# Two GNN layers with LayerNorm on one core: another order of the casts in pass 0, the normalisation of x1 on VectorE, the maximum of the scores by way of TensorE, and the second unit's M3 and M4 around M7

## The chip, the cores and the metric

One core of one Trainium2 chip. The metric is the device time of one execution in microseconds (us); less is better.

## The reference, cut to what matters

Inputs: x (4096 x 256, f32) and adj (4096 x 4096, f32, zeros and ones, symmetric), and small weights. `ln` is a LayerNorm over the 256 columns without affine part.

```python
deg = max(sum(adj != 0, axis=1), 1);  dinv = rsqrt(deg)
x1  = ln(x + relu((dinv * (adj + I) * dinv @ x + x) @ W0 + b0))
h   = x1 @ W_sa;   s_left = h @ a[:256];  s_right = h @ a[256:]
e   = where(adj != 0, exp(-leaky_relu(s_left[:, None] + s_right[None, :], 0.01)), 0)
x_a = (e / (e.sum(1) + 1e-5)) @ h
x_b = adj @ (x1 @ W_gcnb) + b_gcnb
g_a = sigmoid([adj @ x1, x1] @ Wa.T + ba);  g_b = the same with Wb and bb
out = ln(x1 + sigmoid(g_a * x_a + g_b * x_b))
```

`node_degree` of the first layer is `deg`, so the node factors reduce to a division by `deg`.

## The kernel before, in words

A program with one instruction stream for each engine, written out by hand; semaphores (`S[...]`) order the streams, and each stream does its instructions strictly in the order written. The 4096 rows are 32 tiles of 128 (t or n).

**Pass 0 (to 61.9 us).** For each tile t TensorE transposes x (`xt_step`) and multiplies by W0 (`z_step`); ScalarE copies the transpose out of PSUM (`xt_copy`, L523), ScalarE (tiles below `ZACT`) or VectorE copies the product z (`z_copy`, L528, L824). Both split z into two f16 halves `y` (`y_hi` on ScalarE, L535; `y_lo` on VectorE, L851), which waits for a scale (`sx_ready`) that needs all of x. `z_step(t)` waits for `xt_copy(t)`, and z lies in two alternating banks. From the 14th turn on TensorE adds, in each of 16 turns, one row block of adj times y for the first four output tiles (`pass0_rows`, L1324); the other row blocks follow at the end.

**Strips and casts.** adj arrives on SP's queue as 128 strips of 512 KB (L336; 16 strips are a quarter, that is the columns of four output tiles). A strip is cast to one byte an element (`cast`: even strips by ScalarE, L515, odd ones by VectorE, L811). Six strips fit (`RING`): strip s is requested when strip s - 6 is cast. Behind strip `WTS_AT` SP requests all weights of the second layer (`load_weights`, 12 DMAs, four of them of single elements and five broadcasts to all partitions, L307 to L317). Behind strip 21, SP writes the first quarter's codes to DRAM (2 x 1 MB, L324) once strips 0 to 15 are cast; the strips from 22 on are requested behind that.

**Pass 1 (to 328 us).** For each output tile n TensorE sums 64 products (`sum_tile`, L1324; the first four tiles take theirs in pass 0), and between quarters of a tile it transposes an older tile of x1 (`t_step`, L1344) and projects it (`p_step`, L1359). VectorE makes x1 (`degree`, `residual`, `stats`); GpSimd takes the power for the standard deviation (L438) and the shift (L441), ScalarE normalises (`normalize`, L551). ScalarE's `x1t_copy` and `proj_copies` and VectorE's `x1t_lo`, `h_lo` and `forms_lo` split the results into halves.

**Attention.** 16 units of 256 rows. A unit u has seven products after Strassen (M1 to M7, `product`, L1417) for x_b, in banks 0 to 3 (M3 and M5 in 0, M4 and M2 in 1, M1 and M7 in 2, M6 in 3; of unit 0, M5 and M2 in banks 4 and 7), and four chunks of weights times h (`e_chunk`, L1468) for x_a. A chunk c goes: ScalarE's 8 exponentials (`exp_chunk`, L637), VectorE's `mask_chunk` (L1083), ScalarE's `high_chunk` (L646), VectorE's `low_chunk` (L1090), TensorE's `e_chunk`. Products are read by ScalarE (`low_m34`, `low_m1`, `low_m52`, `low_m67`) and VectorE (`middle`: M3 and M4; `middle_m1`; `sums_52`; `sums_67`). TensorE's order of unit 0 to 1 is: M7 of unit 0, then `free_products` (M3, M4 of unit 1, waiting for `sums_52`), `outer_products` (M1, M6), e chunk 0, `onto_products` (M2, M5), e chunk 1, `last_product` (M7 of unit 1, waiting for `middle_m1(1)`), e chunks 2 and 3. The exponentials need `slb`, which needs the maximum of the scores over all rows (`nmax`): GpSimd's `partition_all_reduce`, L450. `row_factors` (L1060 to L1072) gives `slrow` and `arg_ready`, for which ScalarE waits (`rr`, L751).

Of the kernel before, what the change touches and what calls it, by code (L numbers as in the profile page):

```python
# [88 lines left out]
def build(nc, x, adj, W0, b0, Wsa, asa, Wg, bg, Wa, ba, Wb, bb, out):  # L89
# [121 lines left out]
    with ExitStack() as ctx:  # L211
# [196 lines left out]
        def _(pool):  # L408
# [99 lines left out]
        def _(act):  # L508
# [39 lines left out]
            def normalize(n):  # L548

                act.wait_ge(S["shift_ready"], n + 1)  # L550
                act.activation(x1[:, n % X1RING, :], x1[:, n % X1RING, :], ACT.Identity, scale=lnst[:, n % 2, RS],  # L551
                               bias=lnst[:, n % 2, SHIFT]).then_inc(S["x1_ready"], 1)
# [1017 lines left out]
```

## Time and profile before

| | |
|---|---|
| median of 3 runs | 886.35 us (885.96 to 887.74) |
| the profiled execution: its time, its span | 885.95 us, 884.1 us |
| TensorE (PE) busy | 857.5 us, 97% |
| VectorE (DVE) busy | 660.2 us, 75% |
| ScalarE (ACT) busy | 588.4 us, 67% |
| GpSimd (POOL) busy | 208.0 us, 24% |
| mean granted clock of TensorE | 0.991 |

Times are us from the start of the span. A row of a timeline has start, duration, engine, line and operation, output <- inputs, and the idle time of the engine before it with what ended it; consecutive like instructions are merged. TensorE works without a break from 112 to 341 us and from 351 us to 877 us.

### The profile page before, as it was taken

The numbers are of one execution on the slowest core, as the hardware profiler recorded it, in microseconds if no ns is written. First come the engines' busy times: TensorE is split into PE (matmuls) and PEld (weight loads), VectorE is DVE, ScalarE is ACT, GpSimd is POOL, SyncE is SP. The second block draws the span as 40 slices with busy tenths as digits, with TensorE's granted clock in tenths as the row PEclk, the third lists the DMA queues.
The fourth block names the chain that finished last, engine by engine and source line by source line (L and its number), as shares of the span: only waits on it lengthen the run. The fifth ranks groups of instructions, "written<-read, shape, count | busy, mean of one in ns | idle before, by whom it ended". The sixth has DMA issues, their size and how long they took to land.

```text
span 884.1 us, 20483 instructions
## 1 busy us (share of the span) xinstructions
PE 857.5 (97%) x7573; PEld 756.1 (86%) x7573; DVE 660.2 (75%) x1146; ACT 588.4 (67%) x1246; POOL 208.0 (24%) x217
## 2 busy tenths in 40 slices
PE   7998899999999997999999999999999999999996
PEld 6887788888888885888888888888888888888886
DVE  5697465556465457898889988978978978978863
ACT  4664555655555436889877966967967867867832
POOL 1023244343433330110122022032032032032031
PEclk9999999999999999999999999999999999999999
DMA  9789999999989615101220220220220220220001
GB/s 323 226 318 328 340 352 349 382 299 347 364 299 362 217 55 193 54 8 49 79 79 1 77 77 9 68 77 0 77 77 0 77 77 0 77 77 0 25 24 37
DMA packets 67690, 130.02 MB, mean 147 GB/s; under 512 B 6544, under 2 KB 30128, under 8 KB 63152
## 3 DMA queue, kind: packets, MB, share of 16 engines
q1 hardware_dynamic: 58704, 120.87, 39.0%
q10 hardware_dynamic: 8928, 8.38, 2.9%
q8 instruction: 36, 0.59, 0.3%
q14 instruction: 22, 0.18, 0.1%
HBM read 99.87 MB, written 29.36 MB: 146 GB/s over the span
## 4 chain that ended last, share of the span: by engine, by line
PE 90%; DMA 3%; DVE 3%; ACT 1%; SPq 1%; issue 1%; POOL 1%; ACTq 0%; POOLq 0%; DVEq 0%
PE ps L1468 38%; PE ps L1324 22%; PE ps L1417 22%; PE ps L1359 5%; DMA strip<-in_adj_dram 2%; PE ps L1307 1%; DMA xs<-in_x_dram 1%; PE ps L1344 1%; SPq L330 0%; DVE sc L818 0%; PE ps L1296 0%; ACT codes L515 0%; SPq L312 0%; DVE ec L1083 0%; POOL fs L274 0%
## 5 line engine op out<-in xcount | busy, mean ns | idle before, releaser
L1468 PE MATMUL ps<-fb,em 128*128 128x257 f16 x3072 | 347.5, 273 | 0.0
L1468 PEld LDWEIGHTS ps<-fb,em 128*128 128x128 f16 x3072 | 300.5, 98 | 37.4
L1324 PE MATMUL ps<-y,codes 128*128 128x257 f16 x2048 | 238.7, 274 | 0.0
L1324 PEld LDWEIGHTS ps<-y,codes 128*128 128x128 fp8e4 x2048 | 200.9, 98 | 27.2 <-issue 0.3
L637 ACT ACTIVATE ec<-slb,nsb 128x256 f32<-128x256 f32 x512 | 210.8, 496 | 0.1
L1090 DVE SCALAR_TENSOR_TENSOR em<-ec,em 128x2048 f16<-128x2048 f32 x64 | 147.4, 2303 | 24.6 <-ACT em L646 24.6
L646 ACT ACTIVATE em<-ec 128x2048 f16<-128x2048 f32 x64 | 122.0, 1908 | 62.5 <-PE ps L1468 57.1
L1083 DVE SCALAR_TENSOR_TENSOR ec<-ec,pan 128x2048 f32<-128x2048 f32 x64 | 146.7, 2292 | 3.2 <-issue 1.8
L461 POOL TENSOR_TENSOR sc<-sc,sc 128x2 f32<-128x2 f32 x15 | 38.6, 2572 | 245.2 <-DVE sc L1178 245.2
L1417 PE MATMUL ps<-zz,dd 128*128 128x256 f16 x768 | 89.4, 273 | 1.4 <-DVE t L1112 1.4
L1417 PEld LDWEIGHTS ps<-zz,dd 128*128 128x128 fp8e4 x768 | 75.1, 98 | 10.4 <-DVE t L1112 1.7
L515 ACT ACTIVATE codes<-strip 128x1024 uint8<-128x1024 f32 x64 | 66.8, 1048 | 8.6 <-DMA strip<-in_adj_dram 7.0
L455 POOL TENSOR_TENSOR w<-w,bgb 128x512 f32<-128x512 f32 x16 | 27.9, 1744 | 175.8 <-DVE w L1140 156.9
L1417 PE MATMUL ps<-fa,pan 128*128 128x260 f16 x512 | 62.6, 282 | 5.2 <-DVE s L1120 3.9
L944 DVE SCALAR_TENSOR_TENSOR dd<-pan 128x512 uint32<-128x512 uint32 (+2 forms) x85 | 64.2, 815 | 0.0
L551 ACT ACTIVATE x<-x,lnst 128x256 f32<-128x256 f32 x32 | 19.2, 600 | 67.4 <-POOL lnst L441 67.4
L1417 PEld LDWEIGHTS ps<-fa,pan 128*128 128x128 fp8e4 x512 | 51.3, 100 | 13.7 <-issue 4.2
L1417 PE MATMUL ps<-fa,dd 128*128 128x260 f16 x512 | 59.5, 274 | 0.4 <-DVE m L1102 0.4
L438 POOL TENSOR_TENSOR lnst<-lnst,sc 128x1 f32<-128x1 f32 x32 | 27.2, 850 | 137.5 <-DVE lnst L988 134.7
L960 DVE TENSOR_SCALAR lnst<-ps 128x1 f32<-128x1 f32 x32 | 5.0, 157 | 72.2 <-PE ps L1324 72.2
L1417 PEld LDWEIGHTS ps<-fa,dd 128*128 128x128 fp8e4 x512 | 49.9, 98 | 7.3 <-issue 0.6
L1359 PE MATMUL ps<-wps,x1t 128*128 128x256 f16 (+1 forms) x384 | 48.6, 277 | 6.8 <-DVE x1t L950 6.8
(149 smaller groups left out, 808.8 us busy)
## 6 DMA issues: line engine op xcount, KB each, us to landing
strip<-in_adj_dram SPq DMA_DIRECT2D x128, 512.0 KB, 7.1
a_scratch<-codes SPq DMA_DIRECT2D x16, 1024.0 KB, 9.7
pan<-a_scratch SPq DMA_DIRECT2D x16, 1024.0 KB, 5.1
x_scratch<-x ACTq DMA_DIRECT2D x32, 128.0 KB, 5.2
x1r<-x_scratch SPq DMA_DIRECT2D x16, 256.0 KB, 2.8
h_scratch<-hst ACTq DMA_DIRECT2D x30, 136.0 KB, 5.5
out_dram<-ot SPq DMA_DIRECT2D x15, 256.0 KB, 2.2
fb<-h_scratch SPq DMA_DIRECT2D x3, 1088.0 KB, 8.7
```

Of the source, the lines that this page charges most:

```text
L455: pool.tensor_tensor(w[:], w[:], bgb[:].unsqueeze(1).broadcast_to([P, 2, D]), ALU.add).then_inc(S["bias_ready"], 1)
L461: pool.tensor_tensor(sc1[:, RS2], sc1[:, VE2], sc[:, MH2], ALU.pow).then_inc(S["yrstd_ready"], 1)
L515: act.activation(codes_of(s), strip_of(s), ACT.Copy, scale=float(EDGE - NONE), bias=float(NONE)).then_inc(S["cast_act"], 1)
L637: e_ = act.activation(ec[:, c % ER, jj, :], slb[:, slot, :], ACT.Exp, scale=-(1 - SLOPE), bias=nsb[:, jb:jb + 1])
L646: act.activation(em[:, c, 0], ec[:, c % ER], ACT.Copy, scale=MU / EDGE_VAL).then_inc(S["ehigh_ready"], 1)
L944: return dve.scalar_tensor_tensor(out=o, in0=b, scalar=0x7f7f7f7f, in1=a, op0=ALU.bitwise_and, op1=ALU.bitwise_xor)
L1083: dve.scalar_tensor_tensor(out=ec[:, c % ER], in0=ec[:, c % ER], scalar=1.0, in1=pan[:, slot, c * CH:(c + 1) * CH, :].bitcast(F8), op0=ALU ...
L1090: dve.scalar_tensor_tensor(out=em[:, c, 1], in0=ec[:, c % ER], scalar=MU / EDGE_VAL, in1=em[:, c, 0], op0=ALU.mult, op1=ALU.subtract).then ...
L1324: mm = pe.matmul(ACC(n), codes[:, qq % SLOTS, h, jb, e * P:(e + 1) * P].bitcast(F8), y[:, jb, part, 0:YC], start=(jb == 0 and part == 0), ...
L1359: mm = pe.matmul(b, x1t[:, n % 2, x_part, k * P:(k + 1) * P], wps[:, k, w_part, c0:c1], start=(k == 0 and x_part + w_part == 0), stop=(k = ...
L1417: mm = pe.matmul(ps[:, bank, 0:2 * c], a.bitcast(F8), g, start=(p == 0), stop=(p == NP - 1))
L1468: mm = pe.matmul(PH(2 * m + e)[:, 0:HC], em[:, c, e_part, i, e * P:(e + 1) * P], fb[:, jb, h_part, 0:HC], start=(jb == 0 and e_part + h_pa ...
```

## The change

- Pass 0: `ZACT` is 12 (z_copy of tiles 10 and 11 by ScalarE; y starts at turn 12, with 1.5 tiles a turn in place of 2). Casts at ScalarE's turns 11, 13, 14, 16, 17, 19, ... and VectorE's 12, 14, 15, 17, 18, ...: 14 and 13 in pass 0 in place of 11 and 10. The weights are requested behind strip 6 (8 before); VectorE's work on them begins at turn 22 (18 before).
- x1 is normalised by one VectorE instruction, subtract and multiply, that waits for GpSimd's power; GpSimd's shift and ScalarE's instruction go. The same for the last two output tiles.
- ScalarE's part of the forms (`forms_hi`) goes from the end of `proj_copies` behind the next `x1t_copy`. The orders of both engines in tiles 4 and 5 change with the casts.
- `nmax`: TensorE transposes the column of maxima, broadcast, into bank 5 behind M2 of unit 0, and VectorE reduces it; then `slb` ahead of `forms_lo(15)`.
- Unit 0: TensorE does M3 of unit 1, M7 of unit 0, M4 of unit 1. ScalarE's reads of products go between the first exponentials. VectorE's order changes; `row_factors` is split, and `arg_ready` comes behind `mask_chunk(0, 0, 1)`.

```diff
-ZACT = 10
+ZACT = 12
-WTS_AT = 8
+WTS_AT = 6
@@ gpsimd
                 pool.tensor_tensor(ln[:, RS], ln[:, VE], sc[:, MH], ALU.pow).then_inc(S["rstd_ready"], 1)
-                pool.wait_ge(S["rstd_ready"], n + 1)
-                pool.tensor_scalar(ln[:, SHIFT], ln[:, RS], ln[:, 6:7], -1.0, ALU.mult, ALU.mult ...
-            pool.wait_ge(S["nsr_max"], 1)
-            pool.partition_all_reduce(sc[:, NMAX], sc[:, NM], P, RMAX).then_inc(S["nmax_ready"], 1)
@@ split_at
-            upto = lambda i: 0 if i < ZACT else min(i - 1, 2 * (i - ZACT) + 2)
+            upto = lambda i: 0 if i < ZACT else min(i - 1, 3 * (i - ZACT) // 2 + 2)
@@ scalar, pass 0
-                if t >= 11 and t % 2 == 1:
+                if t == ZACT - 1 or t > ZACT and t % 3 != 0:
                     cast(1)
@@ scalar, tiles 0 to 5 (the new order)
+            cast(1); x1t_copy(0); cast(1); proj_copies(0); x1t_copy(1); cast(1)
+            proj_copies(1); x1t_copy(2); forms_hi(0); cast(1); proj_copies(2); x1t_copy(3)
+            cast(1); proj_copies(3); cast(1)
@@ scalar, unit 0
-            low_m34(0)
-            low_m1(0)
             act.wait_ge(S["slb_ready"], 2)
-            exp_chunk(0, 0, 0, first=True)
-            exp_chunk(0, 0, 1, first=True, behind={6: lambda u: low_m52(u, first=True)})
+            exp_chunk(0, 0, 0, first=True, behind={4: low_m34, 5: low_m1, 7: lambda u: low_m52(u, first=True)})
+            exp_chunk(0, 0, 1, first=True, behind={6: lambda u: low_m67(u, first=True)})
             high_chunk(0, 0, True)
-            low_m67(0)
+            act.wait_ge(S["m52_read"], 1)
+            low_m34(1)
             act.wait_ge(S["arg_ready"], 1)
             act.activation(rr[:], tb[:], ACT.Exp).then_inc(S["rr_ready"], 1)
             high_chunk(0, 1, True)
-            low_m34(1)
             exp_chunk(0, 0, 2, first=True)
@@ vector, pass 0
-                if t >= 12 and t % 2 == 0:
+                if t % 3 != 1:
                     cast(1)
@@ vector, tiles
+            def normalize(n):
+                ln = lnst[:, n % 2, :]
+                dve.wait_ge(S["rstd_ready"], n + 1)
+                dve.tensor_scalar(x1[:, n % X1RING, :], x1[:, n % X1RING, :], ln[:, 6:7], ln[:, RS], ALU.subtract,
+                                  ALU.mult).then_inc(S["x1_ready"], 1)
@@ vector, behind the last tile
+            dve.wait_ge(S["nmt_done"], 1)
+            dve.tensor_reduce(sc[:, NMAX], ps[:, 5, P:2 * P], AX, ALU.max).then_inc(S["nmax_ready"], 1)
             ... slb, then forms_lo(NP - 1) and the last differences (these two stood ahead of slb)
@@ vector, unit 0
             middle(0)
             middle_m1(0)
-            row_factors()
-            dve.wait_ge(panel_in[1], 16)
             some_differences(1, 1, DIFF_ORDER[0:2], done=4)
             mask_chunk(0, 0, 0)
+            read_67(0)
+            row_ends()
+            read_52(0, first=True)
-            sums_52(0, first=True)
+            low_chunk(0, 0)
+            add_52(0, first=True)
+            add_67(0)
+            some_differences(1, 1, DIFF_ORDER[2:], done=NPROD + 1)
             mask_chunk(0, 0, 1)
-            sums_67(0)
-            low_chunk(0, 0)
-            some_differences(1, 1, DIFF_ORDER[2:])
+            row_factors()
             middle(1)
             low_chunk(0, 1)
@@ tensor
+            pe.wait_ge(S["nsr_max"], 1)
+            pe.transpose(ps[:, 5, P:2 * P], sc[:, NM].broadcast_to([P, P]), ident[:]).then_inc(S["nmt_done"], 1)
             product(0, "M5", 0, early, bank=FIRST_52[0])
+            pe.wait_ge(S["mid_read"], 1)
+            pe.wait_ge(panel_in[1], 16)
+            product(1, "M3")
             pe.wait_ge(S["mid_read"], 2)
             product(0, "M7")
+            product(1, "M4")
-            free_products(0, 0, 1)
             pe.wait_ge(S["hlo_ready"], T)
             outer_products(0, 0)
+            pe.wait_ge(S["m52_read"], 1)
+            pe.wait_ge(S["slrow_ready"], 1)
```

`row_ends` is h_lo of the last tile and `slrow`; `read_52` and `read_67` are the PSUM reads of `sums_52` and `sums_67`, and `add_52` and `add_67` the rest of them.

## Rows read from the trace of the kernel before

**Rows 1.** TensorE's waits, whole span: us in total, times, longest.
```profile
PE ps L1359 <- DVE x1t L950: 6.8, 3, 3.5
```
**Rows 2.** Timeline of TensorE, pass 0 and tile 4.
```profile
21.57 1.62 PE L1307 MATMUL ps<-w,xt 128*128 128x256 f32 x4 [2.96 <-ACT xt L523]
...
25.45 1.07 PE L1324 MATMUL ps<-y,codes 128*128 128x257 f16 x8
...
56.53 1.04 PE L1324 MATMUL ps<-y,codes 128*128 128x257 f16 x8
...
61.70 14.24 PE L1324 MATMUL ps<-y,codes 128*128 128x257 f16 x128
...
86.52 2.41 PE L1359 MATMUL ps<-wps,x1t 128*128 128x262 f16 x12 [3.53 <-DVE x1t L950]
```
**Rows 3.** Timeline of ScalarE, pass 0 and tile 4.
```profile
20.36 0.91 ACT L535 ACTIVATE y<-zf,sc 128x256 f16<-128x256 f32 x2 [2.64 <-DVE sc L845]
...
44.37 1.06 ACT L515 ACTIVATE codes<-strip 128x1024 uint8<-128x1024 f32 x1 [1.17 <-DMA strip<-in_adj_dram]
...
82.83 1.06 ACT L515 ACTIVATE codes<-strip 128x1024 uint8<-128x1024 f32 x1 [3.54 <-DMA strip<-in_adj_dram]
```
**Rows 4.** Timeline of SP's queue: the first of the weights.
```profile
28.45 0.99 SPq L307 DMA_DIRECT2D wp<-in_L_gnn_W_gcnb_dram  x2
```
**Rows 5.** Chain of waits in order of time, strips 10 and 30: start, duration.
```profile
34.93 9.42 DMA strip<-in_adj_dram
...
78.08 4.72 DMA strip<-in_adj_dram
```
**Rows 6.** L336 from 57.7 to 57.8, strip 22: issue (ns, start), then landing.
```profile
L336 SPq DMA_DIRECT2D strip<-in_adj_dram x1: 1539/1539/1539, 57.8 to 57.8; - x1
...
DMA to landing us min/median/max: 11.2/11.2/11.2
```
**Rows 7.** Timeline of TensorE, first units.
```profile
350.97 6.43 PE L1417 MATMUL ps<-fa,pan 128*128 128x260 f16 x32 [3.94 <-DVE s L1120]
...
360.74 5.44 PE L1468 MATMUL ps<-fb,em 128*128 128x257 f16 x48
...
374.84 1.91 PE L1417 MATMUL ps<-zz,dd 128*128 128x256 f16 x16
```
**Rows 8.** Busy by engine in one stretch; the number behind POOL is the granted clock.
```profile
353.00:354.00 1.00, 1.00 (x7) 0.67 (x6) 0.92 (x2) 0.29 (x1) 0.00 (x0) 0.50 0.00 0
```
**Rows 9.** Timeline of GpSimd, behind the last tile.
```profile
342.59 0.42 POOL L450 PARTITION_ALL_REDUCE sc<-sc  x1 [9.09 <-issue]
```
**Rows 10.** Timeline of ScalarE, first units.
```profile
340.59 0.51 ACT L594 ACTIVATE zz<-fs 128x384 f16<-128x384 f32 x1
...
343.67 5.69 ACT L637 ACTIVATE ec<-slb,nsb 128x256 f32<-128x256 f32 x14
...
357.81 3.30 ACT L637 ACTIVATE ec<-slb,nsb 128x256 f32<-128x256 f32 x8
...
366.94 3.69 ACT L646 ACTIVATE em<-ec 128x2048 f16<-128x2048 f32 x2
```
**Rows 11.** Timeline of VectorE, first units.
```profile
345.43 0.40 DVE L1060 TENSOR_SCALAR rab<-ex,sc 128x32 f32<-128x32 f32 x2
...
347.99 2.28 DVE L1083 SCALAR_TENSOR_TENSOR ec<-ec,pan 128x2048 f32<-128x2048 f32 x1
...
354.06 0.42 DVE L1138 TENSOR_TENSOR s<-s,t 128x256 f32<-128x256 f32 x1
...
357.07 1.89 DVE L944 SCALAR_TENSOR_TENSOR dd<-pan 128x512 uint32<-128x512 uint32 x3
...
371.50 0.29 DVE L1112 TENSOR_TENSOR t<-ps,t 128x128 f32<-128x128 f32 x1
```
**Rows 12.** Timeline of GpSimd, last tile.
```profile
881.07 0.26 POOL L481 TENSOR_SCALAR sc<-sc 128x1 f32<-128x1 f32 x1
```
**Rows 13.** Timeline of ScalarE, last tile.
```profile
881.37 0.60 ACT L794 ACTIVATE ot<-sg,sc 128x256 f32<-128x256 f32 x1 [2.35 <-POOL sc L481]
```

More of the change, by code:

```diff
@@ L546, in _ @@
                 y_hi(t)
[L548 to L552, printed above, removed]
             def x1t_copy(n):
@@ L705, in low_m52, with low_m67 @@
                 a_.then_inc(S["low_m52"], 1)
-            def low_m67(u):
-                gate(act, S["prod_done"], u * NPROD + NPROD, "passed_act")
+            def low_m67(u, first=False):
+                gate(act, S["prod_done"], u * NPROD + NPROD + first, "passed_act")
                 gate(act, S["mid_read"], u * 2 + 2, "passed_act")
@@ L789, in _ @@
                 act.activation(sg[:, e, :], sg[:, e, :], ACT.Tanh, scale=sc[:, HINVA]).then_inc(S["sigmoid_ready"], 1)
-                act.wait_ge(S["yshift_ready"], NPAN + e)
-                if e == 0:
-                    act.wait_ge(out_sent, 16 * (NPAN - 1))
-                c, b = RS2.start + e, SH2.start + e
-                act.activation(ot[:, e, :], sg[:, e, :], ACT.Identity, scale=sc1[:, c:c + 1], bias=sc1[:, b:b + 1]
-                               ).then_inc(S["out_ready"], 1)
         @block.vector
@@ L999, in _ @@
             cast(1)
+            normalize(0)
             head(1)
             x1t_lo(0)
-            cast(2)
+            normalize(1)
+            cast(1)
             head(2)
-            cast(2)
+            h_lo(0)
+            normalize(2)
+            x1t_lo(1)
+            cast(1)
             head(3)
-            h_lo(0)
-            x1t_lo(1)
-            cast(3)
             h_lo(1)
+            x1t_lo(2)
+            normalize(3)
             forms_lo(0)
-            x1t_lo(2)
+            cast(1)
             h_lo(2)
             x1t_lo(3)
+            cast(2)
             head(4)
-            cast(2)
+            h_lo(3)
+            normalize(4)
+            cast(1)
             for n in range(PT + 2, T + 3):
@@ L1036, in _ @@
                 if more:
-                    cast(2)
+                    cast(1)
+                if n - 1 < T:
+                    normalize(n - 1)
+                if more:
+                    cast(1)
                 if T - 2 <= n <= T:
@@ L1054, in _, with row_ends @@
             dve.tensor_scalar(slb[:], slb[:], sc[:, NMAX], None, ALU.min).then_inc(S["slb_ready"], 1)
+            forms_lo(NP - 1)
+            for op in DIFF_ORDER:
+                difference(0, op, NP - 2, NP).then_inc(S["diff_ready"], 1)
+            def row_ends():
+                h_lo(T - 1)
+                dve.wait_ge(S["slt_done"], 1)
+                dve.tensor_scalar(slrow[:], ps[0:T, 5, 0:P], sc[0:T, NMAX], None, ALU.min
+                                  ).then_inc(S["slrow_ready"], 1)
             def row_factors():
-                h_lo(T - 1)
                 for c in range(2):
@@ L1123, in sums_52, with add_52 @@
                 s_.then_inc(S["m52_read"], 1)
+            def add_52(u, first=False):
+                wq = w[:].rearrange("p e (h c) -> p (e h) c", c=P)
                 if not first:
@@ L1207, in attend_tile @@
                 dve.tensor_scalar(one(VE2), two(MV2, 2)[:, e, 1:2], EPS, None, ALU.add).then_inc(S["ystat_ready"], 1)
+                dve.wait_ge(S["yrstd_ready"], NPAN + e)
+                if e == 0:
+                    dve.wait_ge(out_sent, 16 * (NPAN - 1))
+                dve.tensor_scalar(ot[:, e, :], sg[:, e, :], two(MV2, 2)[:, e, 0:1], one(RS2), ALU.subtract, ALU.mult
+                                  ).then_inc(S["out_ready"], 1)
             def dve_step(s, m, nth, ramp=False):
```

90 lines of the change are left out of this document (41 added, 49 removed).

## The prediction, on record before the changed kernel ran

> **What bounds the kernel now.** I read the busy shares first, then TensorE's waits, then the timelines around them. TensorE is busy for 97% of the span and from 112 us on nearly without a break, so a change pays only where TensorE stands still or is slow. The waits show three such places: in pass 0 before 62 us; in tiles 4 to 6, three waits for `x1t_lo` of 6.8 us together [rows 1]; and between pass 1 and the attention, one of 3.94 us with a clock at 0.50 behind it, so that 32 matmuls take 6.3 us (350.97 to 357.24) where the chunk of 48 in 5.44 says 3.6 [rows 7, 8]. The longest of the three in tile 4 (3.53 us, [rows 2]) ends when ScalarE has a strip: its cast at 82.83 waited 3.54 us for DMA with `x1t_copy` behind it [rows 3]. The last tile's chain behind TensorE is the fourth place [rows 12, 13]. Steady state elsewhere gives nothing.
>
> **Pass 0, start.** ScalarE stands before its first y_hi until the scale comes, at 20.36 [rows 3], with `xt_copy(11)` behind it; TensorE waits 2.96 us for that and then runs slowly [rows 2]. With `ZACT` 12 two more tiles pass before y_hi, and TensorE meets the wait only at the first `pass0_rows`, which start at 21.7 (y_hi and y_lo, 0.45 each, after 20.36, and their hand-overs) in place of 25.45 [rows 2]. From there a turn takes 1.97: the 15 turns from 25.45 to 56.53 are 31.1 with 1.1 of waiting and some slack in them [rows 2].
>
> **Pass 0, weights.** The first cast no longer stands behind y_hi and is done near 20, so the weights are requested at 20.2 in place of 28.45 [rows 4]. Strips behind them are late: strip 10, the second behind the weights, was requested at 34.93 and landed 9.42 later, while one on an empty queue needs 4.7 [rows 5]. ScalarE's cast of it shows what follows: 1.17 of idleness and the next `xt_copy` behind it [rows 3]. Now strips 7 and 8 stand there. Moved with the weights, strip 8 lands at 44.35 - 8.25 = 36.1. Ends: 31.4 (requested 26.7, plus 4.7) and 38 (four strips of 1.3 are still in the queue at 20.2). I take 36.1. ScalarE wants it in turn 17, at 29.6; `xt_copy(18)` is then done at 37.4, and TensorE, there at 32.7, does `z_step(18)` at 37.5: a wait of 4.8, where before the weights cost 1.1. The slow stretch behind it costs 1.9 (as 21.57 to 25.45, 3.88 for a turn of 1.97, [rows 2]). `pass0_rows` end at 37.5 + 1.75 + 1.9 + 9 x 1.97 = 58.9; before 57.4.
>
> **Pass 0, end.** Before, ScalarE cast 11 strips here, now 14, up to strip 26. Strips from 22 on are requested behind the two writes of codes. Strip 22 landed at 57.76 + 11.2 = 69.0 [rows 6], 12.6 after strip 21 was requested (56.4); no one wanted it in pass 0. Now strip 21 is requested when VectorE has cast strip 15 (turn 23), about 51.5; strip 22 lands at 64.1, or 1 earlier as fewer strips are ahead: 63. ScalarE wants it in turn 28, near 58. `z_step(29)` starts at 64.4, `z_step(30)` behind strip 24 (65.7, a cast of 1.0 and a copy) at 67.0, and the long sum at 69.0 in place of 61.8 [rows 2]: +7.2. Idle stretches between 60 and 67 slow its start: +1.5 (nothing to 1.9). Together +8.7; if strip 8 comes at 31.4 and DMA never pauses, the strips still let the sum begin no earlier than 61.5, so the lower end is 0; the upper is 10.5.
>
> **Tiles 4 to 6.** In exchange 27 strips are cast before, the rest have landed long before they are wanted, and ScalarE's and VectorE's order puts one cast, not two or three, before each copy TensorE waits for: -6.8 [rows 1], and -1.6 for the slow clock behind the 3.53 (the 12 matmuls at 86.52 take 2.41, at 0.11 each they would take 1.3, and the next lose 0.5, [rows 2]). VectorE now waits in line for GpSimd's power (0.3 to 0.9 a tile) and `forms_hi(0)` for GpSimd's sums ahead of `proj_copies(2)`; I count 1.0 for small waits in tiles 5 and 6 (0 to 2.5). Normalising costs VectorE 0.4 a tile beside 8.6 us of TensorE: nothing in steady state; if VectorE were full it would be 27 x 0.4 = 11. Sum of pass 0 and 1: 8.7 - 8.4 + 1.0 = **+1.3**.
>
> **The maximum.** GpSimd's answer came at 343.01 [rows 9]; a transpose (0.3) and a reduction (0.3) at 339.4 let `slb` be ready at 340.9, and the first exponential starts when `forms_hi(15)` ends, 341.1 [rows 10], in place of 343.67.
>
> The Trainium skill (VectorE: DVE Perf Modes, "Why tensor_reduce can't reduce along partition axis") sends a reduction over partitions to GpSimd, since VectorE's lanes don't talk to each other. Going by that rule alone the exponentials would stay at 343.67 and the forecast would move 2.5 later at most; the row, 4 us from VectorE's maximum to GpSimd's end, speaks for the transpose.
>
> **First units.** An exponential is 0.406 (5.69 for 14, [rows 10]). Chunk 0 with three reads in it is done at 345.5, chunk 1 at 349.1, high part (3.69 for two) at 351.0, low part (2.2, like the mask at 347.99, [rows 11]) at 353.2. TensorE has M3 of unit 1 at 343.9, M7 of unit 0, M4, M1, M6 to 352.9, without a slow clock: its e chunk 0 starts at 353.3 in place of 360.74 [rows 7], 7.4 ahead. That lead is then lost. Behind the low part VectorE has now the sums (1.4: four of 0.42 and a small one, as 354.06), three differences (1.9), the mask of chunk 1 (2.2) and `row_factors` (1.1: 345.43 to 346.8 without `slrow`) [rows 11]: `arg_ready` at 359.8. ScalarE waits for exactly that from 351.3, in front of high part 1 and exponentials 2, for which nothing is missing. Before, that mask and the factors were done by 353.6. Exponentials of chunk 2 start at 359.8 + 0.2 + 1.85 = 361.9 in place of 357.81 [rows 10]. From there to the end of `middle_m1(1)` took 371.79 - 357.81 = 14.0 [rows 10, 11], one chain without slack: exponentials 2 and 3, gates, high part 2 (366.94), low part 2, the two additions. Now it ends at 375.9. TensorE is through e chunk 1 at 369.5 (begun at 364.2), stands 6.4 us at M7 of unit 1, and starts it at 375.9, before at 375.0 [rows 7]: +0.9. The clock falls as after 3.94 us; there it cost 6.3 - 3.6 = 2.7; I take 2.4 (1.6 to 2.8). **+3.3**, ends 0 and +5. Later chunks were ready 5.5 us or more before TensorE came, and VectorE is now 4.1 later, so no further wait.
>
> **Last tile.** GpSimd's 0.26 and its hand-over go, and ScalarE's 0.60 becomes about 0.43 on VectorE [rows 12, 13]: **-0.5**.
>
> **Sum.** 1.3 + 3.3 - 0.5 = +4.1 on the profiled 885.95 (span 884.1 and 1.85 around it): 890.05. That execution lies 0.4 below the median of 886.35, so the median comes to 890.5.
>
> **Rivals.** (1) *Pass 0 isn't held up.* If the weights pass in the shadow of the queue and the writes of codes don't delay strip 22 (strips land near 31.4 and 56), pass 0 ends where it did, and 8.4 of waits in tiles 4 to 6 go: 885.95 - 7.4 + 3.3 - 0.5 = 881.4, or 881.8. For it: the queue ran empty before the weights. Against: 9.42 behind them [rows 5]. It decides when strip 22 lands before 59. (2) *The lead at the first units is kept*, because VectorE reaches `arg_ready` before ScalarE needs it: 890.5 - 3.3 - 7.4 = 879.8. For it: chunk 0 starts early. Against: 8.6 us of VectorE's work stands ahead of it in the new order. (3) *Both losses are half the size* (strip 22 at 60.5, M7 no later and 1 us of slow clock): 886 to 887. (4) *More waits*: VectorE, 4 us late in the units, misses the 5.5 us, and casts wait again for codes in tile 5: +9 to +11, 896.
>
> **How the numbers follow.** No change is within 0.2% (1.8 us). Chances: the forecast 0.50, (1) 0.16, (2) 0.08, (3) 0.15, (4) 0.11. Faster is (1) and (2), 0.24; the same (3), 0.15; slower 0.61. The forecast's own range is 888.3 to 893.5. The range from 882.5 to 895.5 takes in (3) and the near parts of (1) and (4).
>
> **What would show it.** Right: a wait of TensorE near 33 and one near 61 us ended by ScalarE's `xt_copy`, behind casts ended by DMA; the long sum at 69; no wait longer than 1 us from tile 4 to 6; ScalarE idle for 8 us from 351 (all behind pass 0 shifted by 1.3), ended by VectorE; TensorE idle for 6 us before M7 of unit 1, clock 0.50 behind it. Wrong: pass 0 ending by 63, or e chunk 2 of unit 0 starting earlier than 376.

## The result

The changed kernel takes **892.56 us** (median of 5 runs, 892.13 to 894.18); the kernel before took 885.96 us beside it (5 runs, 884.71 to 887.74). The ratio is **1.0078**, with a 95% interval of 1.0061 to 1.0095: slower by about 6.6 us. The forecast was 890.5, that is 4.1 slower. The profiled execution took 892.56 us with a span of 890.3 (before 885.95 and 884.1), so the spans differ by 6.2 us.

Three points of TensorE divide that difference: the start of the long sum that ends pass 0, the start of the late part of unit 0's M3 (the first product behind pass 1), and the end of the span.

| us | before | after | difference | forecast |
|---|---|---|---|---|
| long sum starts | 61.70 | 71.49 | +9.8 | +8.7 (7.2, and 1.5 for a slow start of the sum) |
| late M3 of unit 0 | 342.42 | 344.23 | +1.8 | +1.3 |
| from there to the end | 541.7 | 546.1 | +4.4 | +2.8 |
| of it behind the last group of 192 matmuls of TensorE | | | -0.55 | -0.5 |
| of it the first units | | | +4.9 | +3.3 |

### The profile page after: what moved, and what is told of

It is laid out like the page before. It is cut to its first block, busy times and chain, and to the rows that moved or that the text cites. A ratio compares the mean times of both kernels' runs of the same rounds, so it can differ in the third digit from the quotient of the medians.

```text
span 890.3 us, 20447 instructions
## 1 busy us (share of the span) xinstructions
PE 861.1 (97%) x7574; PEld 758.1 (85%) x7574; DVE 686.0 (77%) x1179; ACT 570.4 (64%) x1214; POOL 183.1 (21%) x182
## 4 chain that ended last, share of the span: by engine, by line
PE 77%; issue 8%; DVE 6%; ACT 5%; POOL 2%; DMA 1%; POOLq 0%; SPq 0%; ACTq 0%; DVEq 0%
PE ps L1498 29%; PE ps L1346 21%; PE ps L1439 18%; PE ps L1381 4%; ACT ec L622 3%; PE ps L1329 3%; ACT em L631 1%; DVE ec L1084 1%; DVE dd L921 1%; DVE em L1091 1%; DMA strip<-in_adj_dram 1%; PE ps L1366 1%; PE ps L1318 1%; POOL zb L431 0%; PE ps L1309 0%
## 5 line engine op out<-in xcount | busy, mean ns | idle before, releaser
L1346 PEld LDWEIGHTS ps<-y,codes 128*128 128x128 fp8e4 x2048 | 200.7, 98 | 28.6 <-DVE y L828 1.8
L449 POOL TENSOR_TENSOR w<-w,bgb 128x512 f32<-128x512 f32 x16 | 26.1, 1634 | 192.4 <-DVE w L1151 192.4
L1439 PE MATMUL ps<-fa,dd 128*128 128x260 f16 x512 | 61.3, 279 | 3.0 <-DVE m L1103 3.0
L1439 PE MATMUL ps<-fa,pan 128*128 128x260 f16 x512 | 60.0, 274 | 1.4 <-DVE zz L907 1.1
L545 ACT ACTIVATE x1t<-ps 128x256 f16<-128x256 f32 x32 | 12.3, 384 | 73.0 <-PE ps L1366 73.0
L438 POOL TENSOR_TENSOR lnst<-lnst,sc 128x1 f32<-128x1 f32 x32 | 25.2, 789 | 149.5 <-DVE lnst L965 149.5
L788 DVE TENSOR_SCALAR codes<-strip 128x1024 uint8<-128x1024 f32 x64 | 50.1, 785 | 1.9 <-DMA strip<-in_adj_dram 1.9
L560 ACT ACTIVATE q<-ps,sc 128x1 f32<-128x1 f32 x32 | 11.2, 351 | 62.9 <-PE ps L1381 62.9
## 6 DMA issues: line engine op xcount, KB each, us to landing
a_scratch<-codes SPq DMA_DIRECT2D x16, 1024.0 KB, 10.2
```

Of the source, the lines that this page charges most:

```text
L788: dve.tensor_scalar(codes_of(s), strip_of(s), float(EDGE - NONE), float(NONE), ALU.mult, ALU.add).then_inc(S["cast_dve"], 1)
L1346: mm = pe.matmul(ACC(n), codes[:, qq % SLOTS, h, jb, e * P:(e + 1) * P].bitcast(F8), y[:, jb, part, 0:YC], start=(jb == 0 and part == 0), ...
L1439: mm = pe.matmul(ps[:, bank, 0:2 * c], a.bitcast(F8), g, start=(p == 0), stop=(p == NP - 1))
```

## The profile after

TensorE's waits over the whole span (us in total, times, longest). They answer to [rows 1]: the three waits for `x1t_lo` are down to 0.3, and others stand in their place.

```profile
PE ps L1329 <- ACT xt L514: 9.9, 5, 4.9
PE ps L1439 <- DVE t L1113: 4.8, 1, 4.8
PE ps L1439 <- DVE m L1103: 3.2, 3, 2.4
```

TensorE's timeline in pass 0 and tiles 4 to 6, the rows that answer to [rows 2]:

```profile
22.34 1.05 PE L1346 MATMUL ps<-y,codes 128*128 128x257 f16 x8 [0.98 <-DVE y L828]
...
37.59 2.08 PE L1329 MATMUL ps<-w,xt 128*128 128x256 f32 x4 [4.16 <-ACT xt L514]
...
66.07 2.08 PE L1329 MATMUL ps<-w,xt 128*128 128x256 f32 x4 [4.92 <-ACT xt L514]
...
68.78 2.66 PE L1329 MATMUL ps<-w,xt 128*128 128x256 f32 x8 [0.21 <-ACT xt L514]
...
103.34 1.50 PE L1381 MATMUL ps<-wps,x1t 128*128 128x262 f16 x12 [0.33 <-DVE x1t L927]
...
108.63 0.44 PE L1366 MATMUL ps<-ident,x 128*128 128x128 f32 x2 [0.28 <-DVE x L971]
```

ScalarE's timeline has the cause of both waits, as [rows 3] had for tile 4. Each stands behind a cast that waited for its strip, strip 8 and strip 22, with the next `xt_copy` queued behind it:

```profile
36.22 1.06 ACT L506 ACTIVATE codes<-strip 128x1024 uint8<-128x1024 f32 x1 [5.86 <-DMA strip<-in_adj_dram]
...
64.70 1.06 ACT L506 ACTIVATE codes<-strip 128x1024 uint8<-128x1024 f32 x1 [5.38 <-DMA strip<-in_adj_dram]
65.67 0.35 ACT L514 COPY xt<-ps 128x256 f32<-128x256 f32 x1
```

SP's queue shows what stood before these two strips. The weights [rows 4] are issued from 20.34 on, and for 7.8 us no strip is requested; the codes are written at 53.15.

```profile
20.34 0.98 SPq L307 DMA_DIRECT2D wp<-in_L_gnn_W_gcnb_dram  x2
...
28.17 24.87 SPq L336 DMA_DIRECT2D strip<-in_adj_dram  x15
53.15 0.88 SPq L324 DMA_DIRECT2D a_scratch<-codes  x2
54.07 6.08 SPq L336 DMA_DIRECT2D strip<-in_adj_dram  x5
```

Busy time by stage of the same kernel (window; PE, PEld, DVE, ACT, POOL busy and count; granted clock, DMA share, GB/s). Two columns matter. TensorE is busy for 3.15 of the 8 us from 58 to 66, while DMA is full (1.02). Then, from 72 to 90, TensorE is full and DMA is at 0.52, since a strip is requested when one is cast, and only four are cast in that time. Before, DMA stood at 0.69 from 50 to 58 and at 0.91 from 72 to 90.

```profile
50.00:58.00 8.00, 8.00 (x60) 6.88 (x59) 6.71 (x22) 5.90 (x13) 0.00 (x0) 1.00 1.00 355
58.00:66.00 8.00, 3.15 (x21) 2.48 (x20) 7.15 (x10) 2.47 (x6) 3.85 (x1) 0.83 1.02 400
...
72.00:90.00 18.00, 18.00 (x166) 16.01 (x165) 15.32 (x44) 3.77 (x9) 4.90 (x7) 1.00 0.52 180
```

TensorE's timeline of the first units, which answers to [rows 7]. The products come at once, e chunk 0 starts at 355.44 in place of 360.74 though pass 1 ended 1.8 later, and then the lead goes: 2.37 us for `middle(1)`, slow matmuls (32 in 5.37, elsewhere 3.71), 4.77 us for `middle_m1(1)`, slow matmuls again. The first slow stretch costs nothing: in e3, below, the same wait of 2.37 is followed by 3.71 us for the 32, the next wait is 6.05, and M7 of unit 1 starts as far behind M3 of unit 0 (34.5 us, here 34.4).

```profile
355.44 5.44 PE L1498 MATMUL ps<-fb,em 128*128 128x257 f16 x48 [0.42 <-DVE em L1091]
...
363.25 5.37 PE L1439 MATMUL ps<-fa,dd 128*128 128x260 f16 x32 [2.37 <-DVE m L1103]
...
378.67 3.57 PE L1439 MATMUL ps<-zz,dd 128*128 128x256 f16 x16 [4.77 <-DVE t L1113]
```

The granted clock behind the longer wait, same columns as above, as in [rows 8]:

```profile
380.00:384.00 4.00, 4.00 (x21) 2.75 (x20) 3.69 (x6) 4.00 (x12) 0.00 (x0) 0.50 0.00 0
```

ScalarE starts the exponentials early (the counterpart of [rows 10]) and is then idle for 9.72 us, until VectorE's last row factor, `tb`:

```profile
342.81 1.69 ACT L622 ACTIVATE ec<-slb,nsb 128x256 f32<-128x256 f32 x4
...
362.62 0.23 ACT L735 ACTIVATE rr<-tb 128x32 f32<-128x32 f32 x1 [9.72 <-DVE tb L1073]
362.75 1.89 ACT L631 ACTIVATE em<-ec 128x2048 f16<-128x2048 f32 x1
```

VectorE, which ScalarE waits for (the counterpart of [rows 11]): low part, sums, three differences, mask of chunk 1, row factors, from 352.89 to 362.58 without a break.

```profile
352.89 2.29 DVE L1091 SCALAR_TENSOR_TENSOR em<-ec,em 128x2048 f16<-128x2048 f32 x1 [1.18 <-ACT em L631]
...
356.37 2.96 DVE L921 SCALAR_TENSOR_TENSOR dd<-pan 128x512 uint32<-128x512 uint32 x3
359.26 2.28 DVE L1084 SCALAR_TENSOR_TENSOR ec<-ec,pan 128x2048 f32<-128x2048 f32 x1
361.46 0.39 DVE L1064 TENSOR_SCALAR rab<-ex,sc 128x32 f32<-128x32 f32 x2
...
362.39 0.19 DVE L1073 TENSOR_TENSOR tb<-tb,ta 128x32 f32<-128x32 f32 x1
```

And the last tile on VectorE, in place of [rows 12, 13]:

```profile
887.77 0.41 DVE L1226 TENSOR_SCALAR ot<-sg,sc 128x256 f32<-128x256 f32 x1 [0.68 <-POOL sc L473]
```

## The experiments

Nine kernels, all edits of the changed one. The times are medians; the three right columns are read from one profiled execution of each kernel. "M3" is the start of the late M3 of unit 0, "rest" the time from there to the end of the span. All results together:

| kernel | median us | ratio to before (95%) | long sum | M3 | rest |
|---|---|---|---|---|---|
| before | 885.96 | | 61.70 | 342.42 | 541.7 |
| changed | 892.56 | 1.0078 (1.0061 to 1.0095) | 71.49 | 344.23 | 546.1 |
| e1: row factors early | 887.51 | 1.0018 (1.0005 to 1.0032) | 70.36 | 342.73 | 540.7 |
| e2: and ScalarE's wait for them later | 885.98 | 1.0004 (0.9992 to 1.0015) | 72.35 | 344.68 | 539.4 |
| e3: casts and weights as before | 882.22 | 0.9956 (0.9943 to 0.9970) | 58.75 | 334.08 | 546.1 |
| e4: codes behind strip 27 | 890.21 | 1.0054 (1.0033 to 1.0075) | 66.22 | 340.98 | 546.0 |
| e5: weights behind strip 16 | 902.97 | 1.0195 (1.0174 to 1.0215) | 72.92 | 354.85 | 546.0 |
| e6: e2 and e3 together | 876.53 | 0.9899 (0.9875 to 0.9923) | 58.42 | 334.79 | 539.5 |
| e7: e3, weights behind strip 6 | 882.15 | 0.9958 (0.9936 to 0.9979) | 58.27 | 333.82 | 546.1 |
| e8: maximum by GpSimd | 895.33 | 1.0111 (1.0087 to 1.0134) | 72.50 | 344.82 | 549.0 |
| e6, codes behind strip 27 | 880.61 | 0.9944 (0.9929 to 0.9960) | 57.62 | 338.52 | 539.5 |

The last column is 546.0 or 546.1 in every kernel with the changed order of unit 0 and its maximum, whatever pass 0 does, and 539.4 or 539.5 in the three with e2's order: the two losses are separate.

**e1.** VectorE does the mask of chunk 1 and the row factors ahead of the sums and the three differences.

```diff
+            mask_chunk(0, 0, 1)
             low_chunk(0, 0)
+            row_factors()
             add_52(0, first=True)
             add_67(0)
             some_differences(1, 1, DIFF_ORDER[2:], done=NPROD + 1)
-            mask_chunk(0, 0, 1)
-            row_factors()
```

> The changed kernel with one edit on VectorE: mask_chunk(0, 0, 1) ahead of low_chunk(0, 0), and row_factors behind that, ahead of the sums and differences. Theory A (in the changed kernel ScalarE stands 9.7 us before arg_ready, and the chain from its exponentials of chunk 2 decides when M7 of unit 1 can start): arg_ready 5 us earlier (near 357.3), exponentials of chunk 2 near 359.3 in place of 364.56, M7 of unit 1 near 373.3 in place of 378.67, e chunk 0 about 0.8 later. Time 892.56 - 5.4 = 887.2, or 2.7 less where the slow clock behind M7's wait goes too: 884.5 to 887.2. Rival B (VectorE has simply too much work in this stretch, so its order is of no account): e chunk 2 starts within 1 us of 382.04, time within 1.5 of 892.6.

Measured: 887.51, and the rest falls by 5.4 us to 540.7. VectorE's last row factor starts 12.7 us behind M3 (355.46 less 342.73), in the changed kernel 18.2 behind it (362.39 less 344.23). TensorE's wait before M7 of unit 1 halves, and M7 takes 2.88 us in place of 3.57 (at full clock 1.91):

```profile
371.73 2.88 PE L1439 MATMUL ps<-zz,dd 128*128 128x256 f16 x16 [2.27 <-DVE t L1113]
```

So the place of the mask of chunk 1 and of the row factors in VectorE's order is the cause of the first units' loss: putting the two forward gives back 5.4 us where 4.9 had been lost. The median is 0.3 above the theory's range.

**e2.** e1, and ScalarE takes the row factors (`rr`) behind the exponentials of chunk 2 instead of in front of high part 1.

```diff
-            act.wait_ge(S["arg_ready"], 1)
-            act.activation(rr[:], tb[:], ACT.Exp).then_inc(S["rr_ready"], 1)
             high_chunk(0, 1, True)
             exp_chunk(0, 0, 2, first=True)
             low_m1(1)
+            act.wait_ge(S["arg_ready"], 1)
+            act.activation(rr[:], tb[:], ACT.Exp).then_inc(S["rr_ready"], 1)
```

> As the kernel before it, and ScalarE waits for arg_ready (rr) only behind the exponentials of chunk 2. Theory A: exponentials of chunk 2 start near 355.8, middle_m1(1) ends near 370, no wait of TensorE at M7 of unit 1 and no slow clock behind it; 10 to 11 us less than the changed kernel: 881.5 to 882.6. Rival B: no better than the kernel before it, since VectorE then is late with the masks: 885 or more.

Measured: 885.98, the rest 539.4, another 1.3 us. That is 3.4 us above the theory's range and in the rival's (885 or more). The medians of e1 and e2 are 1.5 apart and their intervals overlap, so the gain over e1 rests on the last column. M7 now waits 0.69 us and runs at full speed, and M3 of unit 2 comes 9.7 us sooner behind M3 of unit 0 than in the changed kernel (45.0 after 54.7), but later units give back 3 us, in short waits for VectorE (0.87, 1.32, 1.13 between 400 and 445). So the theory is right on M7 and the rival on the units behind it.

```profile
356.81 5.44 PE L1498 MATMUL ps<-fb,em 128*128 128x257 f16 x48 [1.35 <-DVE em L1091]
362.42 3.71 PE L1439 MATMUL ps<-fa,dd 128*128 128x260 f16 x32 [0.17 <-issue]
...
372.10 1.91 PE L1439 MATMUL ps<-zz,dd 128*128 128x256 f16 x16 [0.69 <-DVE t L1113]
```

**e3.** The casts of pass 0, the place of the weights and VectorE's work on them as before (11 and 10 casts), with the missing casts put back into tiles 4 and 5.

```diff
-WTS_AT = 6
+WTS_AT = 8
-                if t == ZACT - 1 or t > ZACT and t % 3 != 0:
+                if t >= 11 and t % 2 == 1:
                     cast(1)
-                if t % 3 != 1:
+                if t >= 12 and t % 2 == 0:
                     cast(1)
...
-            cast(1); x1t_copy(0); cast(1); proj_copies(0)
+            cast(3); x1t_copy(0); cast(2); proj_copies(0)
```

> The changed kernel with the casts of pass 0 as before (11 and 10, every second turn), weights behind strip 8, and three more casts of each engine in tiles 4 and 5. Theory A (the three more casts an engine make pass 0 wait for strips behind the codes; what they save in tile 4 is less): the long sum starts near 59 in place of 71.49, and a wait of 5 to 7 us comes in tile 4, ended by a cast that waits for a strip; end of pass 1 2 to 5 us earlier, time 887.5 to 890.5. Rival B (the number of casts is of no account, the waits of pass 0 come from the weights alone): the long sum starts near 66 and tile 4 has no wait, 887. Rival C (casting early is worth it, what is lost elsewhere): 893 or more.

Measured: 882.22, and the expectation missed on the good side. In pass 0 TensorE has no wait behind a strip (ScalarE's cast of strip 10 waits 1.88 us, in the slack of its turn), the long sum starts 12.7 us sooner, and of that only 2.6 us are lost again in tiles 4 to 6, where I expected 5 to 7 of waiting. TensorE's timeline there, against [rows 2]:

```profile
81.03 1.50 PE L1381 MATMUL ps<-wps,x1t 128*128 128x262 f16 x12 [0.99 <-DVE x1t L927]
...
92.27 1.50 PE L1381 MATMUL ps<-wps,x1t 128*128 128x262 f16 x12 [0.93 <-DVE x1t L927]
```

With 2.7 us in their place, most of the 6.8 us of [rows 1] did not need the third cast in pass 0. What removes them, the changed order of the two engines in tiles 4 and 5, the new normalisation or the earlier start of y, no run separates.

**e4.** Each quarter's codes are written six strips later, behind strip 27 in place of 21.

```diff
+CLATE = 6
-                if s >= RING and (s - RING) % GS == GS - 1:
-                    codes_when_cast((s - RING) // GS)
+                if s >= RING + CLATE and (s - RING - CLATE) % GS == GS - 1:
+                    codes_when_cast((s - RING - CLATE) // GS)
```

> The changed kernel with the codes of each quarter written six strips later (the first behind strip 27, not 21). Theory A (strip 22 lands at 64.7 because the two writes stand ahead of it): strip 22 lands near 58, the wait of 4.92 near 61 us and its slow clock go, the long sum starts near 65 in place of 71.49, no new wait in tile 4; time 885.5 to 887. Rival B (DMA is full until then, so strips 24 and 26 come as late as before whatever the order): the sum starts at 69 or later, 890 or more.

Measured: 890.21, M3 3.3 us sooner, rest unchanged. The time lies where the rival put it (890 or more), but not by the rival's way: the sum starts at 66.22, not at 69 or later, and the wait of 4.92 us near 61 is gone, so at this rate of casts the writes made it. The first wait stays (3.35 us), a wait of 1.93 for VectorE's `z_copy` takes part of the second one's place (one `y_lo` ahead of that copy takes 2.40 us in place of 0.48, beginning at 59.98 beside GpSimd's `partition_all_reduce`, 59.83 to 63.68), and the sum itself takes 15.30 us in place of 14.25 behind it:

```profile
37.41 1.85 PE L1330 MATMUL ps<-w,xt 128*128 128x256 f32 x4 [3.35 <-ACT xt L515]
...
63.47 2.79 PE L1330 MATMUL ps<-w,xt 128*128 128x256 f32 x8 [1.93 <-DVE zf L802]
```

**e5.** The weights behind strip 16; VectorE's work on them four turns later, and its last step, `weight_norm`, behind pass 0.

```diff
-WTS_AT = 6
+WTS_AT = 16
-                if 22 <= t < 26:
-                    weight_column((t - 22) // 2, t % 2)
-                if t == 26:
+                if 26 <= t < 30:
+                    weight_column((t - 26) // 2, t % 2)
+                if t == 30:
                     weight_squares()
-                if t == 30:
-                    weight_norm()
             for t in split_at(T):
                 y_lo(t)
+            weight_norm()
```

> The changed kernel with the second layer's weights requested behind strip 16 instead of strip 6 (VectorE's work on them four turns later). The first of the two stalls of pass 0 (4.16 us, ended by xt_copy behind a cast that waited 5.86 us for DMA) should go, with most of its slow clock: strip 8 then lands before ScalarE wants it. Theory: the 14+13 casts want strips faster than the queue delivers from strip 22 on, so the second stall (4.92 us) grows by about half of what the first gave up: a wait of 6 to 8 near 62, the long sum at 67.5 to 69 (71.5 in the changed kernel), 888.5 to 890.5 us. Rival (the two stalls are independent): second wait 4 to 5, long sum near 65.5, 886.5 us. Rival (the weights were not the cause of the first stall): both waits stay and the time is 892 to 893.

Measured: 902.97, and every theory missed. The first wait goes, as expected, but pass 0 ends no sooner: the stall comes back in three pieces of 10.2 us together, beside the codes. M3 is 10.6 us late, 9 of them from behind pass 0, and that is the edit's own doing: VectorE's next step behind `weight_norm` needs one power from GpSimd. Its input was there at 79.60, but GpSimd starts it at 86.03, the first instruction behind a `partition_all_reduce`. VectorE stands for 7.06 us ahead of tile 4, and TensorE for 6.34. Only the first three rows bear on the question.

```profile
56.51 2.07 PE L1328 MATMUL ps<-w,xt 128*128 128x256 f32 x4 [6.24 <-ACT xt L514]
...
66.63 1.13 PE L1328 MATMUL ps<-w,xt 128*128 128x256 f32 x4 [2.62 <-ACT xt L514]
...
69.35 3.78 PE L1328 MATMUL ps<-w,xt 128*128 128x256 f32 x8 [1.36 <-ACT xt L514]
...
94.39 0.69 PE L1365 MATMUL ps<-ident,x 128*128 128x128 f32 x2 [6.34 <-DVE x L970]
```

```profile
86.03 0.59 POOL L422 TENSOR_TENSOR sc<-sc 128x1 f32<-128x1 f32 x1 [7.35 <-issue]
```

**e7.** e3 with `WTS_AT` at 6, as in the changed kernel. It separates the two edits that e3 undid together.

```diff
-WTS_AT = 8
+WTS_AT = 6
```

> The changed kernel with 11 and 10 casts in pass 0 as before, but the weights still behind strip 6. It separates the two edits that the run with both undone (882.22 us, long sum near 58.8) held together. Theory: the rate of the casts is the cause of both stalls; with every second turn the strips behind the weights come before they are wanted: waits in pass 0 of at most 1.5 us, long sum by 60.5, 882 to 884 us. Rival: the weights behind strip 6 alone make the first stall: a wait of 3 to 5 us between 30 and 40, long sum at 63 to 65, 886.5 to 888.5 us.

Measured: 882.15, the same as e3. Where the weights are requested costs nothing when a strip is cast each turn. A turn is 1.97 us; two casts in three on both engines want a strip every 1.48 us. Strips 7 and 8 are requested right behind the weights and land at about the same time in both kernels: the cast of strip 8 starts at 36.41 here and at 36.22 in the changed kernel. What differs is when ScalarE wants it: at 34.99 here, a wait of 1.42 in the slack of the turn, and at 30.36 there, a wait of 5.86. In e7 no `xt_copy` behind it is late. No run has the higher rate with the weights behind strip 8.

```profile
36.41 1.06 ACT L506 ACTIVATE codes<-strip 128x1024 uint8<-128x1024 f32 x1 [1.42 <-DMA strip<-in_adj_dram]
```

**e8.** The maximum of the scores by GpSimd, and `slb` behind the last differences, as before; no transpose.

```diff
+            pool.wait_ge(S["nsr_max"], 1)
+            pool.partition_all_reduce(sc[:, NMAX], sc[:, NM], P, RMAX).then_inc(S["nmax_ready"], 1)
-            pe.transpose(ps[:, 5, P:2 * P], sc[:, NM].broadcast_to([P, P]), ident[:]).then_inc(S["nmt_done"], 1)
-            dve.tensor_reduce(sc[:, NMAX], ps[:, 5, P:2 * P], AX, ALU.max).then_inc(S["nmax_ready"], 1)
```

> The changed kernel with the maximum of the scores over partitions by GpSimd again, without the transpose, and slb behind the last differences as before. GpSimd's answer comes about 4 us behind VectorE's maximum (340.76 in the changed kernel), so the exponentials start near 345.5 in place of 342.8. Theory: everything in unit 0 hangs on one chain from the first exponential over VectorE's masks to M7 of unit 1, so the 2.7 us arrive nearly whole: M7 waits 7 to 7.5 us, 894.5 to 895.5 us. Rival: VectorE's work in order, not the exponentials, sets the row factors, and the earlier start was worth nothing: 892.5 to 893.2 us.

Measured: 895.33, rest 549.0: 2.9 us more. Reckoned from M3 of unit 0, the first exponential starts 2.6 us later (346.01 less 344.82, in the changed kernel 342.81 less 344.23), after 2.52 us of waiting for `slb`; the low part of chunk 0 starts 3.9 later, and the last row factor 2.9, since the three differences between them are 1.1 us shorter here (1.89 for 2.96; why stands in the last section). So the transpose and the new place of `slb`, undone together, are worth 2.9. How they share it is not shown: in e8 either alone would have held `slb` until about 345.3, since GpSimd's answer is there at 345.27 and the last differences end at 345.44. The Trainium skill (VectorE: DVE Perf Modes, "Why tensor_reduce can't reduce along partition axis") sends such a reduction to GpSimd; here GpSimd's way takes 3.9 us from VectorE's maximum (341.34) to the answer, and the way by TensorE is done 1.3 us behind VectorE's maximum in the changed kernel (340.76 and 342.02), with other work of VectorE in between.

```profile
346.01 1.70 ACT L625 ACTIVATE ec<-slb,nsb 128x256 f32<-128x256 f32 x4 [2.52 <-DVE slb L1052]
```

**e6.** e2 and e3 together.

> The changed kernel with both repairs: the casts of pass 0 and the place of the weights as before (11 and 10 casts, weights behind strip 8), and VectorE's mask of chunk 1 and row factors ahead of the sums, with ScalarE's wait for them behind the exponentials of chunk 2. If the two losses are separate, the ratios multiply: 0.9956 x 1.0004 / 1.0078 = 0.9883, 875.5 us, with the boundary stretch (late M3 of unit 0 to M3 of unit 2) at 45 to 46 us. Rival: what is won at the boundary is partly lost to waits in the next units because ScalarE and VectorE are the bound there: 878 to 880, with three or more waits of about 1 us between 400 and 440.

Measured: **876.53**, 1.0% faster than before (0.9899, 0.9875 to 0.9923) and 16 us faster than the changed kernel. The time is within about 1 us of the product of the ratios (875.5), so the two repairs add up, and the stretch from M3 of unit 0 to M3 of unit 2 is 45.0. The rival's short waits are there as well, three of them (0.89, 1.34, 1.14), at the same places as in e2, which is why the rest is no shorter than e2's:

```profile
398.48 3.71 PE L1439 MATMUL ps<-fa,dd 128*128 128x260 f16 x32 [0.89 <-DVE m L1103]
415.83 3.71 PE L1439 MATMUL ps<-fa,pan 128*128 128x260 f16 x32 [1.34 <-DVE s L1122]
434.73 3.71 PE L1439 MATMUL ps<-fa,dd 128*128 128x260 f16 x32 [1.14 <-DVE m L1103]
```

**e6 with the codes behind strip 27.** Its edit is e4's.

> The kernel with both repairs (876.53 us) and, besides, each quarter's codes written six strips later (behind strip 27, 43, ... instead of 21, 37, ...). In its trace TensorE still waits 3.7 us for x1t_lo in tiles 4 to 6 (1.37, 0.94, 1.40), behind casts of ScalarE that waited 4.15, 1.67, 1.56 and 2.58 us for strips, and DMA is busy there without a break. Theory: the writes only change places with strips; those wanted by tile 4 come up to 5 us earlier, and the waits of tile 4 go (2.3 us, with what the clock gives 2.5 to 3), while those of tile 6 stay: 873.5 to 875 us. Rival: DMA is full from 58 to 112 us whatever the order, so a wait only moves to a later tile: 876 to 877 us.

Measured: 880.61, 4 us slower than e6, outside both expectations. The three waits of tiles 4 to 6 became one of 7.31 us, behind a cast that waited 7.29:

```profile
86.23 2.77 PE L1382 MATMUL ps<-wps,x1t 128*128 128x262 f16 x12 [7.31 <-DVE x1t L928]
```

In both kernels the strip behind the writes is late. In e6 that is strip 22: it lands 9.4 us after its request, ScalarE's cast of it waits 4.15 us and starts at 65.40, under the long sum, when ScalarE has nothing else to do. Here it is strip 28, requested at 69.6 behind the writes at 67.70, landed 10.2 us later and cast at 79.80, and tile 4's `x1t_copy` is queued behind that cast. DMA has room ahead of the writes (windows, same columns as above; from 58 to 72 it is at 1.0 in e6):

```profile
58.00:66.00 8.00, 8.00 (x76) 7.11 (x74) 7.37 (x23) 3.67 (x5) 0.15 (x1) 1.00 0.70 250
66.00:72.00 6.00, 6.00 (x57) 5.37 (x55) 4.70 (x14) 0.14 (x1) 2.58 (x4) 1.00 0.57 213
```

The room is there because the ring is bounded, not because SP was slow: SP waits 7.3 us before it requests strip 27, for VectorE's cast of strip 21, which stands behind the rest of pass 0's work and the first steps of tile 0 on VectorE and starts at 66.51. From 62 to 66 the DMA share is 0.41. The writes, ordered behind strip 27, wait for the same cast.

```profile
66.51 1.29 DVE L789 TENSOR_SCALAR codes<-strip 128x1024 uint8<-128x1024 f32 x2
```

What to take from it: a write has to lie where the strip behind it is not awaited, not merely later, and a later place in the queue can also tie it to a later cast.

## Why the prediction was right, point by point

- **Pass 0, start.** Right: `pass0_rows` start at 22.34 (forecast 21.7), and one of 0.98 stands where the wait of 2.96 was.
- **Pass 0, weights.** Right in place and size: strip 8 is there at 36.2 (36.1), TensorE goes on at 37.59 (37.5) after 4.16 (4.8), with slow matmuls behind. The cause was told by halves. I charged the move of the weights; e7 shows that the move alone costs nothing, and e5 that at the higher rate the waits outlive it (10.2 us in three pieces). The rate of the casts is what makes ScalarE want strip 8 before it can be there.
- **Pass 0, end.** Right in kind, too small by 1.1. Strip 22's cast starts at 64.70 (63), `z_step(29)` at 66.07 (64.4), `z_step(30)` at 68.78 (67.0), the long sum at 71.49 (69.0). The forecast's +8.7 had 1.5 in it for a slow start of the sum; the sum ran at full speed (14.25 us, before 14.24), and the slow matmuls lay ahead of it, in `z_step(29)` to `(31)`. The forecast took 1 us off strip 22 for fewer strips ahead of it, which did not come. e4 shows that the writes of codes are the cause at this rate, e3 and e7 that at a strip a turn the same writes hold up nothing in pass 0.
- **Tiles 4 to 6.** Right: 0.6 us of waits where 6.8 stood. From the long sum to M3, 8.0 us came back, forecast 7.4 (8.4 less 1.0). But e3 shows that I ascribed the gain wrongly: with as few casts in pass 0 as before, most of it comes too. Against e3 the casts cost 12.7 us in pass 0 and bought back 2.6. So M3 at +1.8 for +1.3 is in part luck: the loss in pass 0 was 1.1 larger than forecast, the gain in tiles 4 to 6 0.6 larger, and the second has another cause than I gave.
- **The maximum.** Right: `slb` is ready at 342.65 and the first exponential starts at 342.81; with the 1.8 of pass 1 taken off, 340.9 and 341.0 (forecast 340.9 and 341.1).
- **First units.** Right mechanism, 1.6 too small: +4.9 for +3.3. Less the 1.8, e chunk 0 starts at 353.6 (353.3), `arg_ready` is at 360.8 (359.8), M7 of unit 1 at 376.9 (375.9), and the slow matmuls behind M7's start cost 2.7 (2.4): from M7 to M3 of unit 2 it is 398.94 - 378.67 = 20.27 us, before 392.43 - 374.84 = 17.59. The term that was mis-sized is the three differences, 2.96 us where I took 1.9 from [rows 11] (the chain up to there is otherwise 0.1 off), and the 1.1 us goes through to M7. They grew by the change itself: they meet GpSimd's add of the bias, which in the kernel before came 7 us later, and in e8, with GpSimd's maximum back, they take 1.89 again. A smaller part is my reading of [rows 7]: M7 stands there at 374.84, not 375.0, so the chain alone gave +1.1, not +0.9. Of TensorE's wait I forecast one of 6.4; it came as 2.37 and 4.77, since M2 of unit 1 needs `middle(1)`, which stands behind the row factors too. I had left that wait out.
- **Last tile.** Right: 6.25 us from the end of the last 192 matmuls (884.05) to the end of the span in place of 6.8 (877.30).
- **Rivals.** (1) is out: strip 22 was cast at 64.7, not before 59. Its 881.4 is close to e7's 882.15, but not by the same sum: e7's long sum starts 3.4 us sooner than before, and it has 3.1 us of waits in tiles 4 to 6 where the rival had 1.0. (2) is out in the changed kernel; e2's order keeps part of the lead, 6.7 us of the 10.7 that (2) counted. (3) is out, both losses are somewhat larger than forecast, not smaller. (4) did not come: later waits in the units are 0.8 us in all.

## What to carry to other kernels

A bounded ring of loads can feed only a certain rate across a gap in its queue. To see it beforehand, work out when the first strips behind the gap land (here requested at 28.2 and 28.6, landed 6.7 and 7.6 us later) and when they are wanted at each rate: at a strip every 1.48 us ScalarE came 5.9 us too early, at one every 1.97 1.4. Here one cast more in three lost 10 us, and the place of the weights cost nothing at the lower rate. The place of the writes mattered at both: 2.4 us gained at the higher rate (e4), 4 us lost at the lower one. When an order puts small results (row factors) behind long bulk work, ask which engine waits in order for them: 1.1 us of VectorE's work behind 6 us of sums, differences and mask held ScalarE for 9.7 us and cancelled a lead of 7 us on TensorE. Undo the parts of a change one by one: here one cost 10 us and one 6.6, and with both undone the rest made a kernel 1.0% faster than before. A change that takes work off one engine can move what is left of it: the all-reduce went, GpSimd's next add came 7 us earlier, and it met VectorE at a bad place.

## What the runs showed of the hardware

**Two engines on one operand path.** The same three differences take 1.89 us on VectorE before [rows 11] and 2.96 in the changed kernel, in e1 and in e2 (2.97). In all three of these GpSimd's add of the bias starts 0.26 us behind the first of them. The first keeps its 678 ns; the second, which begins at 356.97, when the add is under way, takes 1761 ns:

```profile
L921 DVE SCALAR_TENSOR_TENSOR dd<-pan x3: 678/683/1761, 356.4 to 358.7; 128x512 uint32<-128x512 uint32 x3
```

```profile
356.63 1.55 POOL L449 TENSOR_TENSOR w<-w,bgb 128x512 f32<-128x512 f32 x1 [22.12 <-DVE w L1151]
```

Before, the same add began 0.08 us behind VectorE's mask, which kept its 2.28 us, and it was the add that took 3.33 (the next mask, begun while the add still ran, took 2.80):

```profile
361.93 3.33 POOL L455 TENSOR_TENSOR w<-w,bgb 128x512 f32<-128x512 f32 x1 [18.92 <-issue]
```

So whichever is under way goes on and the other stands, by these rows (1761 - 680 = 1.08 us of standing for VectorE, 3.33 - 1.55 = 1.8 for GpSimd). The Trainium skill (SBUF — State Buffer, "Who interferes with whom") states this for a VectorE instruction with two inputs in SBUF beside a GpSimd one; the rows agree with it but for one, the add's 0.4 us beside the first difference, of which its 1.55 shows nothing. e8 moves the add away from the differences, and they take 1.89; there the add stands instead, beside a low part that keeps its 2.29:

```profile
360.89 1.89 DVE L924 SCALAR_TENSOR_TENSOR dd<-pan 128x512 uint32<-128x512 uint32 x3
```

```profile
368.29 3.37 POOL L452 TENSOR_TENSOR w<-w,bgb 128x512 f32<-128x512 f32 x1 [23.02 <-issue]
```

**GpSimd behind an all-reduce.** In the kernels with `partition_all_reduce` ahead of the units, that add starts 7.0 us (before, input at 354.94) and 7.3 us (e8, input at 360.97) after its input is there, and the profile shows nothing that it waits for; in the changed kernel, e1 and e2 it starts 0.2 us after it. The power behind the all-reduce of pass 0 came 6.4 us after its input in e5, 4.2 in e4 and 0.75 in e8. No run here tells why.

**A strip behind the writes.** The strip requested behind the two writes of codes lands 11.2 us later before [rows 6], 10.6 in the changed kernel (strip 22), 9.4 in e6 (22) and 10.2 in e6 with the codes behind strip 27 (28). The strip requested just ahead of them in that last kernel needs 5.1.

**Pass 0 varies by itself.** Kernels with the same code up to the units began the long sum at 70.36 (e1), 71.49 (changed), 72.35 (e2) and 72.50 (e8), in one execution each. The kernels with one strip a turn lie at 58.27 to 58.75 (57.62 with the codes behind strip 27). So the first three columns of the table bear readings of several us (e3, e4, e5, e7), not of one or two.
